# Top two from logits tile by tile, prefix sums on TensorE, block owners ahead of slots, plain selections for three blocks, count additions split in three

## The reference

```python
logits = jnp.einsum('bsd,de->bse', x, gate_w) + gate_b      # e0; e1: flat @ router_w.T
probs = jax.nn.softmax(logits, axis=-1)
top_probs, top_idx = jax.lax.top_k(probs, 2)
top_probs = top_probs / jnp.sum(top_probs, axis=-1, keepdims=True)
...
hidden = jax.nn.silu(h1) * h2
expert_out = jnp.einsum('bseh,eho->bseo', hidden, w3)
...
ex = jnp.exp(e - m[dst])                                    # graph attention, over the edges
denom = jax.ops.segment_sum(ex, dst, num_segments=n)
```

## Time and profile before

| what | us |
|---|---|
| median of 3 runs | 1250.96 (1249.01 to 1255.67) |
| profiled execution, its own time | 1260.73 |
| its span | 1259.0 |
| late groups 12 to 31, first instruction of POOL's turn to the last scoring | 243 to 518 |
| `e0`: normalized rows ready to the first `hidden` | 632.8 to 669.4 |
| `e1`: the same | 1040.6 to 1076.4 |

### The profile page before, as it was taken

One profiled execution on the slowest core, in us unless ns is written; L12 is line 12 of the kernel. 1 busy time (PEld: TensorE's weight loads), 2 busy tenths in 40 slices (PEclk: granted clock), 3 DMA queues, 4 the chain that ended last, 5 costly groups with the idle time before them and its releaser, 6 DMA issues.

```text
span 1259.0 us, 19084 instructions
## 1 busy us (share of the span) xinstructions
PE 950.1 (75%) x6438; PEld 825.7 (66%) x6438; DVE 862.1 (68%) x2031; ACT 468.0 (37%) x786; POOL 453.7 (36%) x371
## 2 busy tenths in 40 slices
PE   4377999698898988746327999908982972899991
PEld 1356888598798887546327899805871762788881
DVE  6368369778868889798678788234987757655511
ACT  2045756566866965255111111102540340111110
POOL 1448778877777878400002222040000000111103
PEclk9688999899999999957657999958895995899996
DMA  8942223222223222294017899830000002676752
GB/s 280 292 128 62 54 69 73 59 66 59 67 58 73 62 60 43 51 250 103 1 43 254 291 318 332 324 114 0 1 2 0 1 1 72 229 278 241 268 201 71
DMA packets 58003, 155.94 MB, mean 124 GB/s; under 512 B 23341, under 2 KB 33506, under 8 KB 49674
## 3 DMA queue, kind: packets, MB, share of 16 engines
q1 hardware_dynamic: 25500, 116.31, 27.9%
q0 software_dynamic: 25056, 24.10, 8.6%
q10 hardware_dynamic: 7378, 14.67, 3.5%
HBM read 133.82 MB, written 20.89 MB: 123 GB/s over the span
## 4 chain that ended last, share of the span: by engine, by line
PE 52%; DVE 24%; DMA 8%; issue 7%; POOL 5%; ACTq 2%; ACT 1%; DVEq 0%; POOLq 0%; another core or an unknown queue 0%; SPq 0%
PE bank L704 15%; PE bank L490 9%; PE bank L715 7%; PE bank L654 4%; PE bank L468 4%; DMA pair_scores<-sc_ring,idx_ring 4%; PE bank L452 3%; PE bank L442 3%; DMA arena<-in_exp 2%; POOL arena L1805 2%; PE bank L643 2%; POOL arena L1870 2%; ACTq L1613 2%; PE bank L504 1%; PE bank L770 1%
## 5 line engine op out<-in xcount | busy, mean ns | idle before, releaser
L1860 POOL DMA_INDIRECT arena<-row_tab,ids x42 | 57.7, 1373 | 558.9 <-DVE ids L1381 558.9
L1815 POOL DMA_INDIRECT pair_scores<-sc_ring,idx_ring x160 | 204.7, 1279 | 64.5 <-issue 47.2
L704 PE MATMUL bank<-arena 128*128 128x128 f32 (+1 forms) x1616 | 200.5, 282 | 2.4 <-DMA arena<-in_exp 2.2
L704 PEld LDWEIGHTS bank<-arena 128*128 128x128 f32 (+1 forms) x1616 | 188.3, 190 | 10.8 <-issue 5.8
L1805 POOL DMA_INDIRECT arena<-xl_tab,idx_ring x120 | 158.2, 1319 | 92.5 <-issue 32.6
L715 PE MATMUL bank<-arena 128*128 128x256 f32 (+1 forms) x404 | 99.0, 388 | 0.0
L1585 ACT ACTIVATE late_ohT<-arena 125x875 fp32r<-125x875 f32 x100 | 90.7, 927 | 0.0
L1394 DVE TENSOR_TENSOR arena<-bank,arena 128x512 f32<-128x512 f32 (+2 forms) x76 | 37.2, 508 | 73.9 <-ACT arena L1699 73.8
L1699 ACT ACTIVATE arena<-bank 128x512 f32<-128x512 f32 (+2 forms) x76 | 32.4, 449 | 142.9 <-PE bank L704 142.9
L490 PE MATMUL bank<-late_hi,late_ohT 125*125 125x256 f32 x500 | 84.6, 301 | 0.8 <-DVE arena L917 0.8
L715 PEld LDWEIGHTS bank<-arena 128*128 128x128 f32 (+1 forms) x404 | 72.0, 190 | 16.6 <-issue 9.2
(11 more groups left out here) (312 smaller groups left out, 1988.2 us busy)
## 6 DMA issues: line engine op xcount, KB each, us to landing
arena<-in_exp SPq DMA_DIRECT2D x25, 1024.0 KB, 6.0
arena<-in_exp SPq DMA_DIRECT2D x17, 1364.0 KB
arena<-in_exp0o SPq DMA_DIRECT2D x25, 512.0 KB, 6.3
arena<-pair_scores SPq DMA_DIRECT2D x10, 1093.8 KB
arena<-in_exp1o SPq DMA_DIRECT2D x17, 640.0 KB
pair_scores<-cnt SPq DMA_DIRECT2D x5, 1093.8 KB
pair_scores<-cnt ACTq DMA_DIRECT2D x5, 1093.8 KB
slot_y<-arena ACTq DMA_DIRECT2D x42, 128.0 KB, 5.5
```

What stands on the lines that cost most here:

```text
L704: mm = pe.matmul(banks[1 + 2 * q + buf][0:rows, i * SLOTS:(i + 1) * SLOTS], w_in(s, q, k, m, rows), xsT[:, s, k, :], start=(k == 0), stop= ...
L1815: p.indirect_dma_start(out=pair_scores[which], in_=sc_ring[:, b % 2, j, :], in_offset=None, out_offset=bass.IndirectOffsetOnAxis(ap=idx_ri ...
L1860: p.indirect_dma_start(out=xs[:, q, :], out_offset=None, in_=tab, in_offset=bass.IndirectOffsetOnAxis(ap=ids[:, q, :], axis=0))\
```

## The change

It does five things. (1) In `route`, the maximum and its index are taken from the logits of each tile as soon as they are there; the softmax is computed later, in `shift_logits` and `shares`. The table `pick` is made by one comparison of 160 elements. (2) The sums over tiles are accumulated by PE: five matmuls with a matrix of ones for the totals, then one with `before` and four with ones for the ranks; DVE reads the banks directly. For `e1` the tables are 8 experts wide. (3) `bown_i` is computed before the slots, and SP waits for the second signal of `routed`, not the third. (4) Blocks 0, 1 and 2 (`PLAIN = 3`) have no folds: `select` is one comparison, and `row_nodes` is ten matmuls against `node_id`. PE runs `turn_rows(0)` before `row_nodes(2)`. In a step, `row_nodes(b+3)` comes behind `hidden(b)`, and DVE multiplies before `node_ids` and `select`. (5) `take_counts` is cut in three: its first addition at the end of the second group of a round, the second and third behind the first one-hot column of the third and fourth group. One ACT copy (L1735, scaling of `cnt`) is moved ahead of the gate.

```diff
+PLAIN = 3
...
                 def row_nodes(b, s):
                     pe.wait_ge(sem(name + "_sel"), b + 1)
                     after(pe, sem(name + "_ids"), b)
-                    mm = pe.matmul(banks[7][:, 0:2], sel[:, s, 0, :], one16[:, :], start=True, stop=True)
+                    if isinstance(b, int) and b < PLAIN:
+                        for q in range(2 * T):
+                            mm = pe.matmul(banks[7][:, 0:2], sel[:, s, q, :], node_id[:, q % T, :], start=(q == 0),
+                                           stop=(q == 2 * T - 1))
+                    else:
+                        mm = pe.matmul(banks[7][:, 0:2], sel[:, s, 0, :], one16[:, :], start=True, stop=True)
...
                 def step(b, q):
                     s = q % 2
-                    if not (isinstance(b, int) and b + 3 >= nblk):
-                        row_nodes(b + 3, 1 - s)
                     if not (isinstance(b, int) and b + 1 >= nblk):
                         turn_rows(b + 1, (q + 1) % 4)
                     hidden(b, s)
+                    if not (isinstance(b, int) and b + 3 >= nblk):
+                        row_nodes(b + 3, 1 - s)
...
+                bank, done = group((name, "total"))
+                for t in range(T):
+                    mm = pe.matmul(bank[0:P, 0:NE0], ones16[:, :], pick16[:, t, :], start=(t == 0), stop=(t == T - 1))
+                mm.then_inc(done, 1)
+                bank, done = group((name, "rank"))
+                pe.matmul(bank[0:P, 0:T * NE0], before[:, :], picked, start=True, stop=True, skip_group_check=True)
+                for d in range(1, T):
+                    mm = pe.matmul(bank[0:P, d * NE0:T * NE0], ones16[:, :], picked[:, 0:(T - d) * NE0],
+                                   start=False, stop=True, skip_group_check=True)
...
                 add_fetched(0).then_inc(sem("z_read"), 1)
                 dve.wait_ge(sem("onehot_used"), g - BEHIND)
                 onehot_column(0)
+                if b >= 2:
+                    take_part(segment, ch, b - 1)
...
                 if b == 1:
-                    take_counts(segment, ch)
+                    take_part(segment, ch, 0)
...
+                    read_out(dve, gate_name, t)
+                    own.link(v.max(top8[:, t, :], lg[:, t, 0:ne]))
+                    own.note(v.max_index(topi[:, t, :], top8[:, t, :], lg[:, t, 0:ne]))
...
-                for t in range(T):
-                    for j in range(2):
-                        own.note(v.tensor_scalar(pick[:, j, t, :], iota_e[:, :], topf[:, t, j:j + 1], None,
-                                                 ALU.is_equal))
-                own.fence()
...
+                bank, freed = got(dve, (name, "total"))
+                v.tensor_scalar(nblocks_i[:, :], bank[0:P, 0:NE0], float(SLOTS - 1), None, ALU.add).then_inc(freed, 1)
...
-                sp.wait_ge(sem(name + "_routed"), 3)
+                sp.wait_ge(sem(name + "_routed"), 2)
```

More of the change, by code:

```diff
@@ L729, in experts @@
                 all_free()
-                for b in range(3):
-                    row_nodes(b, b % 2)
+                row_nodes(0, 0)
+                row_nodes(1, 1)
                 turn_rows(0, 0)
+                row_nodes(2, 0)
                 block_steps(pe, nblk, step)
@@ L738, in ranks @@
                 pe.wait_ge(sem(name + "_routed"), 1)
[L739 to L742, removed]
+                picked = pick16[:, :, :].rearrange("p t e -> p (t e)")
+                bank, done = group((name, "total"))
[7 more added lines that the diff above has]
+                                   start=False, stop=True, skip_group_check=True)
+                mm.then_inc(done, 1)
             pe.wait_ge(sem("xn"), 2 * T)
@@ L1319, in route @@
-                own.link(v.tensor_scalar(nblocks_i[:, :], total[:, T - 1, :], float(SLOTS - 1), None, ALU.add))
                 own.link(v.tensor_scalar(nblocks_i[:, :], nblocks_i[:, :], SLOTS.bit_length() - 1, None,
@@ L1329, in route @@
-                own.link(v.tensor_tensor(rank[:, :, :], rank[:, :, :],
-                                         first[:, :].unsqueeze(1).to_broadcast([P, T, NE0]), ALU.add))
-                for j in range(2):
-                    own.link(v.tensor_tensor(pick[:, j, :, :], pick[:, j, :, :], rank[:, :, :], ALU.mult))
-                    own.link(v.tensor_reduce(slotf[:, j, :], pick[:, j, :, :], AX.X, ALU.add))
+                own.link(v.tensor_tensor(eprod[:, 0:ne, 0:ne], before_e[:, 0:ne, 0:ne],
+                                         nblocks[:, 0:ne].unsqueeze(1).to_broadcast([P, ne, ne]), ALU.mult))
@@ new lines, in route @@
+                own.note(v.tensor_reduce(bown[:, 0:nblk], bcmp[:, 0:nblk, 0:ne], AX.X, ALU.add))
+                bank, freed = got(dve, (name, "rank"))
+                v.tensor_tensor(rank[:, :, 0:ne], bank[0:P, 0:T * NE0].rearrange("p (t e) -> p t e", t=T)[:, :, 0:ne],
+                                first[:, 0:ne].unsqueeze(1).to_broadcast([P, T, ne]), ALU.add).then_inc(freed, 1)
+                own.fence()
+                v.tensor_scalar(bown_i[:, 0:nblk], bown[:, 0:nblk], float(ne - 1), None, ALU.min)\
+                    .then_inc(sem(name + "_routed"), 1)
@@ L1398, in step @@
                         ins.then_inc(sem(name + "_mul"), 1)
+                    if not (isinstance(b, int) and b + 3 >= nblk):
+                        node_ids(b + 3, (q + 3) % 4)
+                    if not (isinstance(b, int) and b + 4 >= nblk):
+                        select(b + 4, s)
                     if not (isinstance(b, int) and b == 0):
@@ L1408, in experts @@
                 select(0, 0)
-                owners()
-                for b in range(3):
-                    node_ids(b, b)
-                    select(b + 1, (b + 1) % 2)
+                shift_logits()
+                node_ids(0, 0)
+                select(1, 1)
+                node_ids(1, 1)
+                select(2, 0)
+                shares()
+                node_ids(2, 2)
+                select(3, 1)
                 block_steps(dve, nblk, step)
```

141 lines of the change are left out of this document (77 added, 64 removed).

## The result

The changed kernel took 1248.17 us (median of 13 runs, 1242.57 to 1254.01), the kernel before 1255.07 us on the same chip (13 runs, 1249.01 to 1260.51): ratio 0.9943, interval 0.9923 to 0.9963. That is 7 us faster, where 23 were forecast, and outside the range of 1220 to 1238.

A forecast was written before the change was run, and what follows sets the result against it. No engine was taken to bound the whole kernel. Late groups 4.5, routing of `e0` 8 and of `e1` 10.5 sum to 23 us: 1260.7 to 1237.7 profiled, 1228 us for unprofiled runs; range 1220 to 1238.

The forecast's parts named there:

- Routing of `e0` and of `e1`: Start of both mixtures: first `hidden` 10 and 10.5 us earlier; net gain 8 us in `e0`, 10.5 in `e1`.
- It fits, by 0.2 us.: Block step of `e0`: the new cycle with the selection behind the product takes 5.4 us of the 5.58 us step.
- the block step of `e0` becomes longer: Rival, blocks of `e0`: each 0.1 us above 5.58 is paid in some 21 blocks; 1258 us at 7 us; chance 0.03.
- The giving back in `e0`: First blocks of `e0`: 1.5 us of PE idling before `row_nodes(4)` plus about 0.5 of stalls, 2 of 10 us lost.
- The late groups: Late rounds, count additions split: 2 + 1.8 + 0.7 = 4.5 us gained, bounds nothing and 8 us.
- 0.7 us term: Last late round: a shorter PE hole gives back part of the slow 40 matmuls' 1.4 us, taken as 0.7.
- 1.8 us term: Last late round: one whole count addition, 1.77 us, leaves the stretch ahead of PE's hole.
- the sign of being right: Next profile, late groups: holes of PE ahead of L468 shorter than 2 us.
- The first rival: Late groups give nothing because POOL bounds them: 18.5 us gained in all, 1232.5 us; chance 0.2.
- Its second half: Late rounds: POOL also pays for the split additions, 1248 us at worst, 1240 with half of it; chance 0.06.
- I count no difference: Late rounds: three separate additions delay POOL 0.7 us each, 2.1 us a round, about as much as now.
- the 8 us: Late groups, upper bound of gain: POOL's cap in four rounds with 1.3 as a mean, plus 1.77, plus 1.4.

The follow-up runs named there:

- the late store: Changed kernel with only ACT's step altered: it issues the store of block b-2 instead of b-1 after its SiLU; 1235.80 us, ratio 0.9841.

## Why the prediction was wrong

**Routing of `e0` and of `e1`: right in sum.** Forecast were 10 us sooner for the first `hidden` of `e0` and 10.5 for `e1`. `pick` to `hidden` shrank by 7.9 and 7.0 us; the rest lies ahead of `pick`. Against the moment at which the normalized rows were ready (626.32 and 1034.13 after, 632.84 and 1040.66 before) the first `hidden` came 11.6 and 10.6 us sooner. The parts were off both ways, so that the sum came so close is in part luck: ten matmuls took 0.42 us and not 1.5, the first gathers 5.95 and 6.67 us and not 4.26 (that price was read from a gather of another tile, `slot_y`). That the weights do not bind held.

**The step that failed: "It fits, by 0.2 us."** The cycle of the `e0` step was added up as end of `hidden`, SiLU, product, `ids`, selection: 5.4 of 5.58 us. That path exists, but a shorter list was checked than the one that the engines follow. The diff puts `copy_y(b-1)` behind the selection too; ACT's store waits for it, and SiLU stands behind the store. This loop contains no `hidden` at all and lasts 6.3 to 6.7 us, where 5.58 were forecast to stay. I had asked what is queued behind the moved selection on DVE, and not who waits for that on ACT. With the loop cut at ACT's store alone, 8.5 of the 11.8 us came back; with both orders undone, 13.6. The rival "the block step of `e0` becomes longer" named the right place and the wrong mechanism (a stretched selection), and had a chance of 0.03. Nor did PE wait for the selection, as the sign of being wrong had it: 6.1 us in 12 waits between 663 and 800, while ACT waited 96.9. On average the steps stayed under the rival's 6.7 us, so the change remained faster.

**The giving back in `e0`: right where it was placed.** The forecast had PE idle for 1.5 us ahead of `row_nodes(4)`, and it was, for 1.32 us:

```profile
661.29 0.18 PE L692 MATMUL bank<-one,arena 125*128 125x2 f16 x1 [1.32 <-DVE arena L1412]
```

The step around it took 7.17 us from SiLU to SiLU. It is part of the 11.8 us, and the late store did not remove it.

**The late groups: mis-sized.** 4.5 us were forecast; the stretch shows some 2 us, not clear of its spread, and the timed runs of the split alone none. The rounds wait for POOL for most of their time: from group 12 to 31 its 149 gathers and scatters took 192.5 us before, and with 0.30 us of issue behind each this makes 237 of 250.9 us. At the end of the late groups the chain of the changed kernel has (the answer to the earlier trace rows):

```profile
496.57 2.80 PE bank L471 x10
499.36 5.10 PE bank L493 x40
```

The 40 matmuls behind the hole took 5.10 us instead of 6.14, so that 0.7 us term was fair. The 1.8 us term was not: PE's hole ahead of them is 2.87 us where it was 3.30, and the other four rounds have holes of 1.42 to 4.73 us, though less than 2 us was the sign of being right. Ahead of them the chain now runs through POOL's scatters, not through PE. The first rival ("the late groups give nothing", 0.2) is what happened. Its second half, that the split makes POOL pay more for the additions, hardly did. During a lone addition at 432.47 (1.77 us) POOL's rows are:

```profile
431.71 1.23 POOL L1849 DMA_INDIRECT arena<-xl_tab,idx_ring  x1 [0.30 <-issue]
433.25 2.07 POOL L1859 DMA_INDIRECT pair_scores<-sc_ring,idx_ring  x1 [0.31 <-issue]
435.62 1.24 POOL L1849 DMA_INDIRECT arena<-xl_tab,idx_ring  x1 [0.30 <-issue]
```

The scatter beside it is 0.8 us longer, much as before the split. In 9 of the 15 split additions a scatter beside lasts 1.92 to 2.27 us, which the prediction had named as a sign of being wrong. Yet summed over the 15 additions, POOL's instructions that overlap one took 7.2 us more than the mean of their kind in the changed kernel (6.0 to 9.8 in the eleven kernels with the split), against 5.8 before and 7.6 with the additions together again; without the additions there is no such excess. So POOL pays in every placing, about as much as the 7 us that leaving the additions out gave back, and "I count no difference" was close. That this excess is why they cost 7 us is argued from the sums, not tested by a run. The rule of the Trainium skill ("SBUF — State Buffer", Practical consequences), by which the loser waits for the whole instruction, would allow for up to 1.77 us each; the changed kernel shows 0.7 to 1.1 in those nine places, and the split alone cost nothing that the runs can tell. One bound in this part does not follow from its own rows: the 8 us take 1.3 us as the mean of caps that had been read as 1.2 and 3.2.

**The sum.** By the stages the change took 7.9 - 11.8 + 3.6 + 7.0 + 0.9 = 7.6 us from the first `pick` on, some 4 us ahead of it in the routing of `e0`, and at most 2 us in the late groups: 11 to 13 us. The timed runs say 7 us, 5 to 10 by the interval. In the profiled executions the time of the first `pick` varies from 635.1 to 644.2 us among kernels that are alike up to there, more than what is missing; the difference stays open.

## What to carry to other kernels

When instructions change places in one engine's list, write down the whole loop of one step over all engines, every copy and store in it, and look for the longest circle; a circle need not contain the engine that seems to bound the kernel. An instruction that waits for a late one delays all that stands behind it on its own engine: a store that nobody is in a hurry for goes last, or one step later. Before giving a crowded stretch its price, leave the work out altogether once: here that run would have capped the late groups at 7 us of 24 in the trace, and at 5 by the timed runs.

The best of these kernels, both step orders of before with PLAIN = 5, takes 1235.6 us (0.9851 of before, where the changed kernel has 0.9943); the late store alone, 1235.8, cannot be told from it.

## What the runs showed that was not expected

- The landing time of the same gather in the blocks of `e0` went with the place of `node_ids` in DVE's step: medians of 4.1 to 4.8 us behind the multiplication, 5.7 to 7.2 ahead of it.
- The 15 additions on DVE cost POOL about the same wherever they stood: an excess of 5.8 and 7.6 us together, 6.0 to 9.8 us split. Only leaving them out removed it.
- Ten matmuls of 2 columns into one bank took 0.42 us together, while a lone one takes 0.17 to 0.18.
- The load of ACT's table ahead of the first SiLU takes 1.28 us, and shows only when SiLU is late. The Trainium skill ("ScalarE: Activation LUTs", What ACT_TABLE_LOAD costs) states the same figure for the load, 1283 ns. It adds about 1380 ns of drain for each switch of the table; no run here shows that: SiLU starts 0.02 us behind the end of the load, and the load 0.02 us behind the copy ahead of it.
